# A recommendation model on one core: another order of matrix work in the first chunk, a bias added by a matmul, a shorter index chain

## The reference, cut to what matters

```python
def mlp(x, Ws, bs):
    for W, b in zip(Ws, bs):
        x = relu(x @ W + b)
    return x

bot_out = mlp(dense_x, [bw0, bw1, bw2], [bb0, bb1, bb2])          # 512 x 13 -> 512 -> 256 -> 128
gathered = stack([emb[t][sparse_x[:, t]] for t in range(26)], 1)  # 512 x 26 x 128
features = concatenate([bot_out[:, None, :], gathered], 1)        # 512 x 27 x 128
Z = einsum('bnd,bmd->bnm', features, features)
x = concatenate([bot_out, Z[:, LI, LJ]], 1)                       # 128 + 351 pair products
y = mlp(x, [tw0, tw1, tw2, tw3, tw4], [tb0, tb1, tb2, tb3, tb4])  # 479 -> 1024 -> 1024 -> 512 -> 256 -> 1
```

## Time and profile before

| | us |
|---|---|
| median of 3 runs | 212.52 |
| lowest, highest | 211.9, 214.16 |
| span of the profiled execution, first to last instruction | 179.6 |
| busy: PE, POOL, DVE, ACT | 167.0, 100.7, 82.2, 66.3 |

### The profile page before, as it was taken

How to read it: one execution, slowest core, us unless ns; L and a number is a source line. 1 busy time by engine, 2 the same in 40 slices (tenths; PEclk the granted TensorE clock), 3 DMA queues, 4 the chain that set the end, 5 groups by cost and what they waited for, 6 DMA issues and landing times.

```text
span 179.6 us, 3315 instructions
## 1 busy us (share of the span) xinstructions
PE 167.0 (93%) x1354; PEld 128.6 (72%) x1354; DVE 82.2 (46%) x177; ACT 66.3 (37%) x103; POOL 100.7 (56%) x112
## 2 busy tenths in 40 slices
PE   1999999899599994999999999989999999999993
PEld 1335557568377783798878889977888898788992
DVE  3202588955165756374452346343506625411422
ACT  0576748664143655133033253112504611110211
POOL 3777776777777777777777777767772000000000
PEclk9999999999999999799999999999999999999999
DMA  4999972434499733242232244422223120000000
GB/s 97 369 337 391 390 239 58 100 66 89 89 302 374 285 79 86 54 100 68 44 61 51 52 105 85 93 46 62 46 59 72 24 53 7 4 0 0 0 0 4
DMA packets 10124, 19.93 MB, mean 111 GB/s; under 512 B 5639, under 2 KB 5771, under 8 KB 9981
## 3 DMA queue, kind: packets, MB, share of 16 engines
q1 hardware_dynamic: 6636, 12.89, 22.0%
q0 software_dynamic: 3328, 6.82, 16.7%
q10 hardware_dynamic: 144, 0.00, 0.0%
HBM read 18.26 MB, written 1.44 MB: 110 GB/s over the span
## 4 chain that ended last, share of the span: by engine, by line
PE 71%; DMA 10%; POOL 8%; issue 4%; SPq 2%; DVE 2%; ACT 2%; POOLq 0%; DVEq 0%; ACTq 0%
PE acc L799 14%; PE acc L803 13%; PE acc L800 12%; POOL rows L420 8%; PE feat L781 6%; PE turned L944 5%; PE feat L763 5%; DMA rows<-in_emb,index 3%; PE turned L881 3%; DMA pairs<-pair_scratch 3%; DMA pair_scratch<-dots 3%; PE acc L829 2%; PE acc L938 2%; PE feat L938 2%; DMA v<-in_bw 1%
## 5 line engine op out<-in xcount | busy, mean ns | idle before, releaser
L420 POOL DMA_INDIRECT rows<-in_emb,index x104 | 99.5, 957 | 34.4 <-issue 30.0
L799 PE MATMUL acc<-w1h,y_split 128*128 128x512 f32 x64 | 27.9, 436 | 0.0
L803 PE MATMUL acc<-w1h,y_split 128*128 128x512 f32 x64 | 26.1, 407 | 0.0
L800 PE MATMUL acc<-w1l,y_split 128*128 128x512 f32 x64 | 25.5, 399 | 0.0
L444 ACT COPY featT<-feat 128x512 f32<-128x512 f32 x16 | 17.6, 1097 | 14.4 <-PE feat L763 14.3
L457 ACT ACTIVATE y_split<-turned 128x512 fp32r<-128x512 f32 x16 | 9.7, 606 | 35.1 <-PE turned L881 35.1
L651 DVE SCALAR_TENSOR_TENSOR y_split<-turned,y_split 128x512 fp32r<-128x512 f32 x16 | 11.1, 692 | 18.7 <-ACT y_split L457 18.7
L799 PE MATMUL acc<-w2h,y_split 128*128 128x256 f32 x64 | 18.8, 294 | 0.0
L803 PE MATMUL acc<-w2h,y_split 128*128 128x256 f32 x64 | 18.0, 281 | 0.0
L763 PE MATMUL feat<-ident,rows 128*128 128x128 f32 x104 | 15.3, 277 | 2.7 <-DMA rows<-in_emb,index 2.7
L800 PE MATMUL acc<-w2l,y_split 128*128 128x256 f32 x64 | 17.8, 279 | 0.0
(11 more groups left out here) (107 smaller groups left out, 255.6 us busy)
## 6 DMA issues: line engine op xcount, KB each, us to landing
w1r<-in_w SPq DMA_DIRECT2D x8, 512.0 KB, 13.8
w2r<-in_w SPq DMA_DIRECT2D x4, 512.0 KB, 6.0
rows<-in_emb,index POOLq DMA_INDIRECT x104, 3.0
w0r<-in_w_pairs SPq DMA_DIRECT2D x3, 512.0 KB, 7.8
top<-in_top_rows SPq DMA_DIRECT2D x1, 1024.0 KB, 12.1
pair_scratch<-dots SPq DMA_DIRECT2D x8, 104.0 KB, 2.3
pair_scratch<-dots SPq DMA_DIRECT2D x8, 71.5 KB
v<-in_bw SPq DMA_DIRECT2D x1, 512.0 KB, 3.6
```

The costliest lines, as they stand in the source:

```text
L420: pool.indirect_dma_start(rows[:, i, :], None, table, bass.IndirectOffsetOnAxis(ap=index[:, c, i:i + 1], axis=0)).then_inc(s_gather[LOTS * ...
L799: nc.tensor.matmul(dst, ah, wh, start=first, stop=False)
L800: nc.tensor.matmul(dst, ah, wl, start=False, stop=False)
L803: return nc.tensor.matmul(dst, al, wh, start=False, stop=end)
```

## The change

First chunk only (c = 0):

- PE. Before, the rest of layer 1 (steps 6 and 7 of its second half) stood behind the turns of lots 2 and 3 of the next chunk's half 1, and layer 2 began behind the pair products. After, layer 1's rest comes first, then steps 0 and 1 of layer 2, lot 2's turn, steps 2 and 3, lot 3's turn, the turn of layer 1's second half, two steps of layer 2's second half, and only then the pair products. Five `keep_going` matmuls stand at the chunk's end.
- ACT. `split_hi(1, 0, 0)` moves ahead of lot 2's copy, `split_hi(1, 0, 1)` ahead of the copies of the pair products.
- DVE. `split_lo(1, 0, 0)`, `copy_out(1, 0, 1)` and the last weight piece's rest come ahead of lot 3's copy, `split_lo(1, 0, 1)` ahead of the copies of the pair products.

Last chunk: layer 3's bias is added on PE by a matmul of one row (a row of ones times the bias, plain float32), so DVE's L671 goes. The ones are set by a GpSimd memset behind the last gather. The last output row is made by DVE (`last_out`) and no longer by ACT.

Index chain: 3 DVE instructions a part, no longer 4.

```diff
@@ scalar, chunk(c)
                     if c == 0:
                         weight_hi(UPPER + 3)
+                        split_hi(1, c, 0)
                     feature_lot(c + 1, 1, 2)
-                split_hi(1, c, 0)
+                if c == 0:
+                    split_hi(1, c, 1)
+                else:
+                    split_hi(1, c, 0)
                 if not end:
                     dots_out(c + 1, 1)
-                split_hi(1, c, 1)
+                if c > 0:
+                    split_hi(1, c, 1)
                 layer2_out(c, 0)
...
             layer2_out(CHUNKS - 1, 1)
-            layer4_out(CHUNKS - 1)
@@ vector, indices
-                dve.wait_ge(s_chain, 3 * n + 1)
-                nc.vector.tensor_tensor(tmp, tmp, raw, ALU.add).then_inc(s_chain, 1)
-                dve.wait_ge(s_chain, 3 * n + 2)
-                nc.vector.tensor_scalar(tmp, tmp, 0.0, float(VOCAB - 1), ALU.max, ALU.min).then_inc(s_chain, 1)
+                dve.wait_ge(s_chain, 2 * n + 1)
+                nc.vector.scalar_tensor_tensor(out=tmp, in0=raw, scalar=float(VOCAB - 1), in1=tmp, op0=ALU.min,
+                                               op1=ALU.add).then_inc(s_chain, 1)
                 dve.wait_ge(s_base, PER_GATHER)
-                dve.wait_ge(s_chain, 3 * n + 3)
-                nc.vector.tensor_tensor(part(index), tmp, part(index_base), ALU.add).then_inc(s_index, 1)
+                dve.wait_ge(s_chain, 2 * n + 2)
+                nc.vector.scalar_tensor_tensor(out=part(index), in0=tmp, scalar=0.0, in1=part(index_base), op0=ALU.max,
+                                               op1=ALU.add).then_inc(s_index, 1)
@@ vector, end
+            def last_out():
+                dve.wait_ge(s_l4, CHUNKS)
+                dve.wait_ge(s_out, 16 * (CHUNKS - 1))
+                nc.vector.tensor_scalar(y4[:], turned[1][0:1, 0:P], bias4, 0.0, ALU.add, ALU.max).then_inc(s_y4, 1)
@@ tensor
+            def bias3_in(c):
+
+                pe.wait_ge(s_top, 16)
+                pe.wait_ge(s_ones, 1)
+                nc.tensor.matmul(layer3_block(c), ones, bias3[0:1, :], start=False, stop=False)
@@ tensor, layer3(c)
                 layer3_lo(c, 0)
+                if c == CHUNKS - 1:
+                    bias3_in(c)
                 layer3_hi(c, 1)
@@ tensor, chunk(c)
                 layer2(c, 1, range(6, 8))
+                if c == 0:
+                    keep_going(acc_of(1, 0), 5, w0h[:, 0, :])
```

More of the change, by code:

```diff
@@ L169, in rec_kernel @@
         ident_r = xl[:, 0, :]
+        ones = rows[0:1, 0, :]
         y3 = y_evac[:, 1, 0:T3]
@@ L191, in rec_kernel @@
             sem, ("sparse_in", "dense_in", "small_in", "w3_in", "top_rows_in", "ones_set"))
+        s_ones = sem("ones_row_set")
         s_v = [sem(f"bottom_weights{i}_in") for i in range(3)]
@@ L428, in _ @@
                         gather_lot(c, h, j)
+            pool.wait_ge(s_ft, HALVES * LOTS * (CHUNKS - 1) + 1)
+            pool.memset(ones, 1.0).then_inc(s_ones, 1)
         @block.scalar
@@ L670, in layer3_out @@
                 dve.wait_ge(s_l[3], c + 1)
-                nc.vector.tensor_tensor(y3, layer3_block(c), bias3, ALU.add).then_inc(s_y3, 1)
-                dve.wait_ge(s_y3, c + 1)
-                nc.vector.scalar_tensor_tensor(out=y3, in0=y3, scalar=0.0, in1=w4, op0=ALU.max, op1=ALU.mult,
+                if c == CHUNKS - 1:
+                    before = layer3_block(c)
+                else:
+                    before = y3
+                    nc.vector.tensor_tensor(y3, layer3_block(c), bias3, ALU.add).then_inc(s_y3, 1)
+                    dve.wait_ge(s_y3, c + 1)
+                nc.vector.scalar_tensor_tensor(out=y3, in0=before, scalar=0.0, in1=w4, op0=ALU.max, op1=ALU.mult,
                                                accum_out=y4c[:, 0:1]).then_inc(s_y4c, 1)
+            def last_out():
+                dve.wait_ge(s_l4, CHUNKS)
+                dve.wait_ge(s_out, 16 * (CHUNKS - 1))
+                nc.vector.tensor_scalar(y4[:], turned[1][0:1, 0:P], bias4, 0.0, ALU.add, ALU.max).then_inc(s_y4, 1)
             for n in range(0, 3):
@@ L733, in chunk @@
                     feature_lot(c + 1, 1, 1)
-                    if c == 0:
-                        weight_lo(UPPER + 2)
+                if c == 0:
+                    weight_lo(UPPER + 2)
+                    split_lo(1, c, 0)
+                    copy_out(1, c, 1)
+                    weight_lo(UPPER + 3)
                     feature_lot(c + 1, 1, 3)
-                split_lo(1, c, 0)
-                copy_out(1, c, 1)
-                if not end:
+                    split_lo(1, c, 1)
                     dots_out(c + 1, 1)
-                if c == 0:
-                    weight_lo(UPPER + 3)
-                split_lo(1, c, 1)
+                else:
+                    if not end:
+                        feature_lot(c + 1, 1, 3)
+                    split_lo(1, c, 0)
+                    copy_out(1, c, 1)
+                    if not end:
+                        dots_out(c + 1, 1)
+                    split_lo(1, c, 1)
                 copy_out(2, c, 0)
@@ L751, in _ @@
             layer3_out(CHUNKS - 1)
+            last_out()
         @block.tensor
@@ L813, in bot_parts, with keep_going @@
                     bot_times_w0(part_banks[g], g // 2 + 1, g % 2).then_inc(s_pre, 1)
-            def keep_going(bank, times):
+            def keep_going(bank, times, w=wbh):
                 for _ in range(times):
-                    nc.tensor.matmul(bank[:], wbh[:, 0:P], wbh[:, 0:NB], start=True, stop=True)
+                    nc.tensor.matmul(bank[:], w[:, 0:P], w[:, 0:NB], start=True, stop=True)
             def hi_back(n):
@@ L1032, in chunk @@
                 turn(1, c, 0)
-                if not end:
+                if c == 0:
+                    layer1(c, 1, 6)
+                    layer1(c, 1, 7)
+                    layer2(c, 0, range(0, 2), hi_ready(1, c, 0))
                     turn_lot(c + 1, 1, 2)
+                    layer2(c, 0, range(2, 4))
                     turn_lot(c + 1, 1, 3)
-                layer1(c, 1, 6)
-                layer1(c, 1, 7)
-                if not end:
+                    turn(1, c, 1)
+                    layer2(c, 1, range(0, 2))
                     dots_of(c + 1, 1)
-                layer2(c, 0, range(0, 2), hi_ready(1, c, 0))
-                turn(1, c, 1)
-                layer2(c, 0, range(2, 4))
-                layer2(c, 1, range(0, 4))
+                    layer2(c, 1, range(2, 4))
+                else:
+                    if not end:
+                        turn_lot(c + 1, 1, 2)
+                        turn_lot(c + 1, 1, 3)
+                    layer1(c, 1, 6)
+                    layer1(c, 1, 7)
+                    if not end:
+                        dots_of(c + 1, 1)
+                    layer2(c, 0, range(0, 2), hi_ready(1, c, 0))
+                    turn(1, c, 1)
+                    layer2(c, 0, range(2, 4))
+                    layer2(c, 1, range(0, 4))
                 layer2(c, 0, range(4, 8), hi_ready(1, c, 1))
```

## The result

| | before | after |
|---|---|---|
| median (us) | 213.34 (4 runs, 211.9 to 214.94) | 217.18 (4 runs, 215.41 to 217.85) |
| ratio after / before | | 1.0214, 95% interval 1.0127 to 1.03 |
| span of the profiled execution | 179.6 | 214.0, own time 217.31 |

The change makes the kernel slower by 2.1%. I had forecast 211.5 us in a range of 210.0 to 213.3. The time of after's profiled execution lies 3.3 us above its span, not 32.9. So the trace of before (span 179.6) was of an execution unlike the ones that gave 212.52.

The account below looks back on a forecast made before the run. PE's own work and its few waits, chiefly the first chunk's stall for gathered rows, were taken as the bound. Savings of 0.65 + 0.31 + 0.07 = 1.03 us gave span 178.6, plus 32.9 outside: 211.5 us, range 210.0 to 213.3.

Parts of the forecast that it names:

- the new order, step by step: First chunk, PE: laid out from layer 1's turn at 67.96 to the pair products at 74.0.
- The new wait for DVE's low part: First chunk, layer 2's third product: PE waits 0.93 us, until DVE's low part is ready at 70.94.
- the pair products' end sets layer 0: Chunk 1's layer 0 starts 6.73 us after the pair products' end, as long as PE's remaining work fits in.
- The pair products start at 74.0 and not at 74.63: 0.63 us gained: First chunk: the new order gains 0.63 us at the pair products, so chunk 1 starts near 82.6.
- the sum's term of 0.65 us saved: First chunk's new order: 0.65 us saved in all, with a little for ACT's earlier rounding; bounds 1.6 and -0.4.
- the lower bound of the first chunk: First chunk's saving: -0.4 us at worst, if DVE's moved work ran 1 us late.
- the 0.5 us of slack: First chunk: ACT's and DVE's copies of lots 2 and 3 come 0.5 us before the pair products at 74.0.
- My argument against this rival: Before chunk 0's layer 0, PE idled 1.94 us and the next matmul took 0.50, its full-clock length after a wait.
- The gathers: Rival, chunk 1 or 2: PE waits for late gathered rows and loses what it won; 212.0 us, chance 10%.
- The rival that ends slower: Clock falls in PE's 1.8 us idle time before chunk 1's layer 0: costs 1.6 us, 213.1 us, chance 12%.
- 0.31 + 0.07 saved: Last layers: bias matmul replaces DVE's addition, net 0.31 us (bounds 0.1, 0.46); last output on DVE, 0.07 us (-0.06, 0.14).
- With the 32.9 us outside the span: Base: 32.9 us outside the span, added to the forecast span of 178.6 to give 211.5 us.

Follow-up runs that it names:

- e4: The whole change, unedited, against the kernel before on one chip: 182.36 us beside 181.30, ratio 1.0056.
- e1: The change without its end and index parts (first chunk's new order plus keep_going matmuls) against the kernel before: 182.51 us beside 180.98, ratio 1.011.
- f1: The kernel before, unchanged, run again beside itself: 213.58 us beside 213.39, ratio 1.0007, span 210.7.
- e0: The kernel before, unchanged, run again beside itself: 181.19 us beside 180.98, ratio 1.0026, span 179.1.
- e6: First chunk's new order without the five keep_going matmuls, end and indices as before, against the kernel before: 182.36 us beside 181.30, ratio 1.0049.
- e5: Kernel before with only layer 1's six matmuls moved ahead of the turns of lots 2 and 3 in the first chunk: 180.24 us beside 181.30, ratio 0.9946.
- e2: Kernel before with only the bias matmul, the ones' memset and the last output on DVE: 181.12 us beside 180.98, ratio 1.0012.
- e3: Kernel before with only the three-instruction index chain: 180.77 us beside 180.98, ratio 1.0003.
- e7: Kernel before with only the five keep_going matmuls at the first chunk's end: 181.04 us beside 181.30, ratio 0.9997.
- f2: The whole change, unedited, against the kernel before on another chip: 215.63 us beside 213.39, ratio 1.0079.
- e11: Kernel before plus e5's edit, the bias matmul early in the last chunk, last output on DVE and short index chain: 213.38 us beside 212.99, ratio 1.0063.

## Why the prediction was wrong

**Right: the new order, step by step.** From layer 1's turn to the pair products I had laid out 74.0 - 67.96 = 6.04 us. Measured: e4 74.30 - 68.27 = 6.03, after 93.29 - 87.31 = 5.98. The new wait for DVE's low part: 0.93 forecast, 0.80 (e1), 0.73 (e4), 0.71 (after) measured. And that the pair products' end sets layer 0: 6.73 us forecast, 103.57 - 96.95 = 6.62 in after, 6.87 in e4. In f1 it is 8.13, since there PE's own work fills the time until layer 0.

**Wrong: what was subtracted from.** On the chips that gave the measured times (213 us), and on the others too, the step that failed is "The pair products start at 74.0 and not at 74.63: 0.63 us gained". The 6.67 us of before (67.96 to 74.63) held a wait of 1.81, one of 0.67 and 1.43 us of slow clock. In e0 the same way is 73.62 - 69.18 = 4.44 us, in f1 89.89 - 87.21 = 2.68. So the new order starts the pair products 1.6 us later, or 3.3, where I had them 0.63 earlier, and the sum's term of 0.65 us saved became a stage 1.6 to 2.1 us longer (e1, e4, e6 against e0), or 2.75 (after against f1). I took one execution's stall and slow clock for properties of the kernel. That 2.5 us of layer 2 go ahead of the pair products and that PE then waits for them, I had said myself.

The stall's end follows POOL's pace (on the 181 us kind lot 3 lands between 71.3 and 72.7 in all five traces of the old order), its beginning is where PE comes from its own work, and that moves: PE's turn stands at 68.0 in the first trace, at 69.2 in e0 and at 87.2 in f1. The half clock stood elsewhere in e0. Both should have been in the sum at a bound of zero as well.

**Wrong: the lower bound of the first chunk.** I gave "-0.4, if DVE's moved work ran 1 us late"; with the 0.5 us of slack that I had counted, 1 us late leaves even 0.2 gained. The bound that mattered is the stage without a stall: 18 matmuls and a turn ahead of the pair products plus the new wait, 2.07 + 0.45 + 0.93 = 3.45 us by my own terms, against 3.30 measured between f1 and after. In f1 PE was busy with layer 2 until 101.83, so only 1.74 us of the 3.40 came through at layer 0.

**Missed: layer 0 waits more than once.** I followed the pairs only to layer 0's first block. From there to layer 3 it is 2.64 us in e0 and 2.65 in f1, but 3.17 in e1 and 3.70 in after, since the later blocks wait in turn (0.41 and 1.00). That is 0.5 to 1.05 us on top.

**The rivals.** In the changed kernel the clock did not fall in the new idle time: e4 has no slow stretch in its span (mean 1.00) and is slower all the same. My argument against this rival was weak, though. I read from the first matmul behind the wait of 1.94 us, 0.50 us long, that the clock holds. In six traces (e0, e1, e2, e3, e5, e7) a half clock of 3.4 us follows that same wait of 1.9 to 2.0 us, but it begins up to 2.1 us after the wait's end: the first matmul tells little. In e6 it follows the wait before layer 0 of chunk 1. The Trainium skill, "TensorE: Matmul & The Clock Gate", section "HAM oscillation — how this bites in real kernels", has waits between bursts send the array back to the slow clock, so that the next burst starts cold. These seven traces agree that the clock falls behind a wait, though in six of them matmuls pass at full clock first. The wait of 1.94 us in the first trace and in e6 and the waits of 2.15 and 1.65 us in e4 were not followed by it. The gathers had nothing to take back in the change; in e5, where something was won, PE waits 0.47 us for gathered rows at 104.64, so this rival was sound. The rival that ends slower was there, but with the wrong mechanism; a rival that said "the stall is not in every execution" was missing.

**The end.** Forecast 0.31 + 0.07 saved; measured none. The bias matmul holds PE for 0.62 us, not 0.43 (0.33 of it is issue before the next weight load), and it began 0.15 us before the high part was ready, not 0.28: 0.47 sticks out and not 0.15. My lower bound was wrong as well: twice 0.43 would have been 0.12 lost (0.46 - 0.58), not 0.1 gained. The two weight loads of one row took 0.29 us together, as long as two of 128 rows (0.30), so there was indeed no discount. DVE's last output took 0.34, over the 0.29 I took, against ACT's 0.36. **The indices**: 0 forecast, 0 measured (1.0003).

**The base.** "With the 32.9 us outside the span" was wrong: it was the difference between two kinds of execution. Outside the span lie 2 us. A span 15% under the time (179.6 against 212.52) should have been read as a trace that does not belong to the times.

**How much is explained.** On chips of the 181 us kind: stage +1.6 to 2.1 us against e0, medians +1.5 (e1) and +1.1 (e4, e6). On those of 213 us: stage +2.1 (f2) and +2.75 (after), outside the span +0.4, medians +2.2 (f2 over its 213.39; 1.7 by its ratio) and +3.8 (4.5 by its ratio). For the first measurement 0.7 to 1.4 us stay open; four runs a side, with 2 to 3 us between lowest and highest, do not resolve them. The order alone (e1, e6) was measured on the 181 us kind only.

## What to carry to other kernels

Before moving work into a stall, find out whether the stall is the kernel's or one execution's: ask what fixes its beginning and its end, and put it in the sum once at its size and once at zero. Fill a hole only with what was queued behind it (e5, and even that pays only where the hole is), and let the step on which the next stage hangs follow at once; every matmul put in front of it is paid when the hole is not there. When span and time do not match, the trace is of another kind of execution, and nothing that depends on when data arrive can be read from it.

## What the runs showed of the hardware

The same program ran at two speeds: 181.0 and 181.3 us on two chips, 213.0 and 213.4 us on two others (and 213.3 in the first measurement), with two profiles of the kernel before at 179.1 and 210.7. Each chip was measured at one time only, so whether it is the chip or the occasion is not shown. Part of the difference is at half clock: 23.8 us of f1's span and 3.4 of e0's are at the 1.2 GHz level. Another part is in the dense bursts of pair products, 64 short matmuls with a weight load each. In e0 such a burst takes 1.94 us. In after, the one of half 0 of chunk 1, and below it the issue idle time of all bursts (total, times, longest):

```profile
78.21 0.42 PE L805 MATMUL feat<-featT 128*59 128x54 f32 x3 [1.20 <-issue]
79.63 0.25 PE L805 MATMUL feat<-featT 128*59 128x54 f32 x1 [1.00 <-issue]
80.33 1.94 PE L805 MATMUL feat<-featT 128*59 128x54 f32 x33 [0.46 <-issue]
...
PE feat L805 <- issue: 13.9, 25, 1.2
```

It runs from 73.4 to 82.3. f1's begins 4.1 us later and ends at the same time, e11's ends at 80.5, and all the others of this kind end between 81.9 and 82.8, wherever they began between 73.3 and 78.8. In the later burst of after 50 matmuls pass at full pace, and then 4 or 5 every 0.72 us. Bursts that end together and runs of even length look as if PE's place in its program, and not its data, were held to a pace, but this was not tested. The Trainium skill, "Runtime: NRT & Kernel Launch", section "Instruction fetch mechanics", says that engines stream their instructions from a small memory that is refilled by blocks, and that the cost is mostly hidden; if the pauses are a starved stream, that does not hold for these bursts, and no run here decides it.

The stretches at the 1.2 GHz level last 3.4 us on the 181 us kind. One stands behind PE's wait before layer 0 of chunk 0 in e0, e1, e2, e3, e5 and e7 (it begins at 47.6 to 49.9), one at the waits for gathered rows in the first trace (71.1) and in e3 (72.0), and one behind the wait before layer 0 of chunk 1 in e6 (84.0). e4 has none. On the other chips there are four to seven, of 3.4 or 6.8 us.

The plain float32 matmul of one row and 256 columns held PE for 0.62 us, and DVE took 0.34 us for 1 x 128 elements from PSUM.
